# 16-wide attention written out as straight code, with keys and queries turned into planes per group

## The reference

```python
qkv = einsum('bsh,oh->bso', layernorm(x), w_qkv) + b_qkv     # 8 x (4 + 2) x 16
q, k = _rope(q, cos, sin), _rope(k, cos, sin)
scores = einsum('bqhd,bkhd->bhqk', q, k) * SM_SCALE           # SM_SCALE = 1/16
scores = where(mask, scores, finfo.min)                       # block mask; causal at this length
probs = softmax(scores)
ctx = einsum('bhqk,bkhd->bqhd', probs, v)
x = x + einsum('bsh,oh->bso', ctx, w_dense) + b_dense
```

## Time and profile before

| what | before |
|---|---|
| median of 3 runs (lowest, highest) | 3000.42 us (2997.31, 3000.43) |
| the profiled execution | 2997.02 us, span 2995.0 us |
| busy in the span | PE 2652.2 us (89%), PE weight loads 1793.2, DVE 1907.5, ACT 1514.3, POOL 822.2 |
| mean granted PE clock | 0.945 of 2.4 GHz |
| L0a: projection / first minima / groups | 21.3 to 108.8 / 108.8 to 135.5 / 135.5 to 446.5 us |
| L1b: the same | 2148 to 2235.8 / 2235.8 to 2262 / 2262 to 2575.6 us |

### The profile page before, as it was taken

The page is one execution under the profiler, slowest core; times in us unless marked ns, Lnnn a source line. Parts: engine busy times, 40 slices in busy tenths (PEclk is TensorE's granted clock), DMA queues, the critical chain, the costliest instruction groups (busy, mean ns, idle before and its releaser), DMA issues. The chain is left out here.

```text
span 2995.0 us, 46427 instructions
## 1 busy us (share of the span) xinstructions
PE 2652.2 (89%) x14824; PEld 1793.2 (60%) x14886; DVE 1907.5 (64%) x3382; ACT 1514.3 (51%) x2540; POOL 822.2 (27%) x777
## 2 busy tenths in 40 slices
PE   6789988886999999999999987999578888778995
PEld 4444434454888888888888864666344444345663
DVE  5666642444777787777777766677556666166774
ACT  4466661222555555555555541566265666324663
POOL 1200000104343443445335301455120000003552
PEclk9799998997999999999999988999788999979998
DMA  2100000001000000000000023988500000029887
GB/s 76 71 1 0 0 1 16 19 17 46 19 22 22 22 22 18 22 22 26 15 22 25 8 92 135 297 201 199 144 1 1 0 0 0 11 107 322 211 201 197
DMA packets 68154, 196.92 MB, mean 66 GB/s; under 512 B 9040, under 2 KB 9936, under 8 KB 62608
## 3 DMA queue, kind: packets, MB, share of 16 engines
q1 hardware_dynamic: 46928, 145.44, 14.2%
q0 software_dynamic: 21056, 49.30, 8.7%
HBM read 154.33 MB, written 40.37 MB: 65 GB/s over the span
## 5 line engine op out<-in xcount | busy, mean ns | idle before, releaser
L1315 ACT ACTIVATE L1a_ph<-single 128x512 fp32r<-128x512 f32 (+3 forms) x384 | 174.2, 489 | 180.4 <-PE single L1402 179.7
L698 DVE TENSOR_REDUCE L1b_least<-single 128x1 f32<-128x512 f32 (+3 forms) x304 | 191.2, 660 | 107.9 <-PE single L520 75.9
L698 DVE TENSOR_REDUCE L0a_least<-single 128x1 f32<-128x512 f32 (+3 forms) x304 | 191.1, 660 | 106.9 <-PE single L520 75.5
L1456 DVE TENSOR_TENSOR L1a_pl<-single,L1a_ph 128x512 fp32r<-128x512 f32 (+3 forms) x384 | 199.5, 549 | 52.7 <-ACT L1a_ph L1315 52.0
L1472 DVE SCALAR_TENSOR_TENSOR x<-single,L1a_rinv,x 128x512 f32<-128x512 f32 x256 | 189.5, 745 | 58.4 <-PE single L1066 58.4
L1306 ACT ACTIVATE L1a_probs<-pair,L1a_least 128x128 f32<-128x128 f32 (+7 forms) x256 | 190.0, 744 | 72.0 <-DVE L1a_least L1450 70.8
L1450 DVE TENSOR_REDUCE L1a_least<-pair 128x1 f32<-128x128 f32 (+7 forms) x256 | 190.8, 750 | 43.3 <-PE pair L1391 42.6
L1283 POOL TENSOR_TENSOR L1a_swapped<-L1a_swapped,L1a_sin 128x512 f32<-128x512 f32 x80 | 129.8, 1622 | 303.7 <-ACT L1a_swapped L1347 303.7
L409 ACT ACTIVATE L1b_probsT<-pair 128x896 f32<-128x896 f32 (+2 forms) x192 | 151.2, 811 | 67.4 <-PE pair L539 48.1
L409 ACT ACTIVATE L0a_probsT<-pair 128x896 f32<-128x896 f32 (+2 forms) x192 | 151.2, 811 | 65.9 <-PE pair L539 46.5
L1402 PE MATMUL single<-ident,L1a_probs 128*128 128x128 f32 x1152 | 169.0, 274 | 1.4 <-ACT L1a_probs L1306 1.4
(11 more groups left out here) (517 smaller groups left out, 7052.1 us busy)
## 6 DMA issues: line engine op xcount, KB each, us to landing
L1f_wd<-in_L1f_w SPq DMA_DIRECT2D x48, 512.0 KB, 4.3
L1g_wd<-in_L1f_w SPq DMA_DIRECT2D x48, 512.0 KB, 4.2
L1a_raw<-in_L1a_w SPq DMA_DIRECT2D x80, 256.0 KB, 2.6
L1f_store<-in_L1f_w SPq DMA_DIRECT2D x16, 1024.0 KB, 7.9
L1g_store<-in_L1f_w SPq DMA_DIRECT2D x16, 1024.0 KB, 8.4
sum<-L0a_pad_row SPq DMA_DIRECT2D x2, 2304.0 KB, 11.7
sum<-x SPq DMA_DIRECT2D x16, 256.0 KB, 2.9
x<-sum SPq DMA_DIRECT2D x16, 256.0 KB, 4.7
```

What stands on the lines that cost most here:

```text
L698: dve.tensor_reduce(a.least[:, part, qt, first:first + heads], g.bank(4 + f % 2)[:, 0:heads * w].rearrange("p (j k) -> p j k", j=heads), A ...
L1315: act.activation(p_tile(ph, u, i), turned_bank(u, i), ACT.Copy).then_inc(p_high, 1)
L1456: dve.tensor_tensor(p_tile(pl, u, i), turned_bank(u, i), p_tile(ph, u, i).bitcast(F32), ALU.subtract)\
```

## The change

1. **Straight code.** The hardware loops of the groups become Python loops, so every instruction stands in the program with constant operands.
2. **Two rounded parts in place of three bf16 parts.** Queries and keys are held as a float32r (rounded fp32) high part and a float32r rest. In `qs` a head has 64 columns: high, rest, high, two columns for the row extreme, zeros. In `ks` the key has 64 columns: high, high, rest, ones; with 64 zero columns on each side.
3. **Planes per group.** The projection stretch no longer builds or turns any stack. POOL builds `qs`, `ks` for group kv+2 (`build`), PE turns four tiles of two heads at once into bank 7 (`turn_plane`, 4 matmuls of 128 columns) and ACT copies the bank (`plane_copy`, 128x512). Per group and half of the tokens: two planes K, two planes Q, and later two planes M, which are the Q planes again, now with the row extremes in them. So 12 planes a group take the place of the 40-head stacks and the 8 rows.
4. **Whole arrays, zeros in the other half.** A query plane holds two heads, one in each half of the 128 partitions; the key plane for head j has the key in the half j % 2 and zeros in the other, so the matmul picks one head.
5. **Minima and scores.** Fills now take heads (0, 2) and (1, 3) where two fit in a bank, so 40 fills a group in place of 38; the fills stand behind the two score matmuls of their step, and masks are put a matmul later where they can be. The row extreme has two parts in place of three.
6. **First stretch.** The list `START16` has 4 planes, then the 40 fills of group 0 with 14 more planes among them: the other planes of group 0 and those of group 1.

```diff
-            n = max(1, min(GH, HALF // w))
-            out += [(qt, part, j, n, w) for j in range(0, GH, n)]
+            pairs = ((0, 2), (1, 3)) if 2 * w <= HALF else ((0,), (1,), (2,), (3,))
+            out += [(qt, part, heads, w) for heads in pairs]
...
+TURNS_AT = {
+    1: ("M", 0, 0, 1), 3: ("M", 0, 1, 1), 5: ("K", 2, 0, 0), 6: ("K", 2, 1, 0), 8: ("Q", 2, 0, 0), 10: ("Q", 2, 1, 0),
+    13: ("M", 1, 0, 0), 15: ("M", 1, 1, 0), 16: ("K", 2, 0, 1), 18: ("K", 2, 1, 1), 20: ("Q", 2, 0, 1), 22: ("Q", 2, 1, 1),
+}
...
-        self.qkT = sb("qkT", [P, NQK, T], BF16)
+        self.qs = sb("qs", [P, SETS, NT, GH, ROWS16], F32R)
+        self.ks = sb("ks", [P, 2, NT, 3, ROWS16], F32R)
+        self.qT = sb("qT", [P, SETS, 2, T], F32R)
+        self.kT = sb("kT", [P, SETS, 2, T], F32R)
...
+                def build(kv, c):
...
+                    pool.wait_ge(a.roped, (c + 1) * BLK)
...
+                    pool.tensor_tensor(ks[:, :, 0:HD], k, like(1, HD)[:, :, 0, :], ALU.mult).then_inc(a.stack_high, 1)
+                    pool.tensor_tensor(qs[:, :, :, 0:HD], q, like(GH, HD), ALU.mult).then_inc(a.stack_high, 1)
+                    pool.tensor_tensor(ks[:, :, HD:2 * HD], k, like(1, HD)[:, :, 0, :], ALU.mult).then_inc(a.stack_high, 1)
+                    pool.tensor_tensor(qs[:, :, :, 2 * HD:KF], q, like(GH, HD), ALU.mult).then_inc(a.stack_high, 1)
+                    pool.tensor_tensor(qs[:, :, :, KF:KM], like(GH, 2), like(GH, 2), ALU.subtract).then_inc(a.stack_high, 1)
...
+                    pool.tensor_tensor(ks[:, :, 2 * HD:KF], k, ks[:, :, 0:HD].bitcast(F32), ALU.subtract)\
+                        .then_inc(a.stacked, 1)
+                    pool.tensor_tensor(qs[:, :, :, HD:2 * HD], q, qs[:, :, :, 0:HD].bitcast(F32), ALU.subtract)\
+                        .then_inc(a.stacked, 1)
...
+                def plane_copy(kind, kv, p, c):
...
+                    act.wait_ge(a.plane_turned, PLANE[kind, kv, p, c])
+                    act.activation(to, g.bank(7), ACT.Copy).then_inc(a.plane_copied, 1)
...
-                for t in range(NT):
+                for t in range(2, NT):
+                    qkv(t)
                     if t + 2 < NT:
-                        qkv(t + 2)
-                    turn_stack(t)
-                    if t + 4 < NT:
-                        turn_row(t + 4)
-                pe.wait_ge(a.stackT_copied, 5 * NT)
+                        turn_row(t + 2)
...
+                def turn_plane(kind, kv, p, c):
+
+                    bank_7_free((kind, kv, p, c))
...
+                    for i in range(BLK):
...
+                        mm = pe.matmul(g.bank(7)[:, i * P:(i + 1) * P], rows.rearrange("p j d -> p (j d)"), a.ident[:, :],
+                                       start=True, stop=True)
+                    mm.then_inc(a.plane_turned, 1)
...
+                        mm = pe.matmul(outs[n], a.kT[:, b, j % 2, kt * P:(kt + 1) * P],
+                                       a.qT[:, b, j // 2, c * HALF + q:(c + 1) * HALF], start=True, stop=not diagonal)
...
-                with pe.Fori(0, NKV - 1) as kv:
-                    group(kv, True)
-                group(NKV - 1, False)
```

More of the change, by code:

```diff
@@ L209, in groups @@
     return [(c, kt) for c in range(2) for kt in range(0, BLK * (c + 1), 2)]
-FILLS, GROUPS = fills(), groups()
-NF, NG = len(FILLS), len(GROUPS)
-NF0 = sum(f[0] < BLK for f in FILLS)
+GROUPS = groups()
+NG = len(GROUPS)
 NU = NG * GH
@@ L248, in heads16_plan, with next_fill @@
[L248 to L258, removed]
+    left, order, plan = fills(), [], []
+    total, given = sum(len(h) * w for _, _, h, w in left), 0
+    def next_fill(parity):
+        block = [f for f in left if f[0] // BLK == left[0][0] // BLK][:GH]
+        f = next((f for f in block if f[2][0] % 2 == parity), block[0])
+        left.remove(f)
+        order.append(f)
+        return len(order) - 1
@@ new lines, in heads16_plan @@
+    for n in range(NU):
+        i, j = divmod(n, GH)
+        now = []
+        while len(left) > 2 and given + len(left[0][2]) * left[0][3] <= total * (n + 1) / NU:
+            now.append(next_fill((j + 1 + len(now)) % 2))
+            given += len(order[-1][2]) * order[-1][3]
+        plan.append(("seen", i, j, now))
+        if i == 0 and j == 2:
+            plan.append(("values",))
+        if i and j == 1:
+            plan.append(("weigh", i - 1))
+            if i == GROUPS_BEFORE[1]:
+                plan.append(("copy", 0))
+        if n in TURNS_AT:
+            plan.append(("plane", *TURNS_AT[n]))
+        if i == GROUPS_BEFORE[1] and j == 3:
+            plan.append(("turn", 0))
@@ new lines, in heads16_plan, with heads16_start @@
+    plan += [("fill", next_fill(0)), ("weigh", NG - 1), ("copy", 1), ("fill", next_fill(1)), ("turn", 1)]
+    return plan, order
+PLAN16, FILLS = heads16_plan()
+NF = len(FILLS)
+NF0 = sum(f[0] < BLK for f in FILLS)
+def heads16_start():
+    first = [("K", 0, 0, 1), ("K", 0, 1, 1), ("Q", 0, 0, 1), ("Q", 0, 1, 1)]
+    later = [("M", 0, 0, 0), ("M", 0, 1, 0)] + [(k, 1, p, c) for c in range(2) for k in "KQ" for p in range(2)]
+    out = [("plane", k, 0, p, 0) for k in "KQ" for p in range(2)]
+    for f in range(NF):
+        out.append(("fill", f))
+        if f < NF0 and f % 3 == 2 and first:
+            out.append(("plane", *first.pop(0)))
+        if f >= NF0 + 2 and f % 3 == 2 and later:
+            out.append(("plane", *later.pop(0)))
+    return out + [("plane", *p) for p in first + later]
@@ L452, in _ @@
+                for kv in range(NKV):
+                    for s in PLAN16:
+                        if s[0] == "seen":
+                            exponentials(kv, s[1], s[2])
+                        elif s[0] == "plane" and kv + s[2] < NKV:
+                            plane_copy(s[1], kv + s[2], s[3], s[4])
+                        elif s[0] == "copy":
+                            context_copy(kv, s[1])
                 for t in range(NT):
```

484 lines of the change are left out of this document (229 added, 255 removed).

## The result

The changed kernel took 3007.18 us (median of 18 runs, 2996.28 to 3017.53) against 2997.40 us for the kernel before on the same chips: a ratio of 1.0026, 95% interval 1.0015 to 1.0037. It is 0.3% slower, where 2942 us were forecast. Its profiled execution took 3003.43 us (span 3001.7), and by the steps of the sum (2938.5 us for a profiled execution) that is 65 us longer than forecast.

What follows compares the result with a forecast made beforehand. PE was taken as nearest to the bound in the groups. Projection savings less costlier minima and groups gave -27.7 and -30.8 us, so 2997.0 - 58.5 = 2938.5, plus 3.4 to the median: 2942 us, range 2895 to 2985.

Steps and rivals of the forecast that it cites:

- Projection: Before the first fill: tiles 5.6 us apart, then four planes in 5.4 us; first fill 35.5 us earlier in L0a.
- First minima: Group 0's first minima: planes make PE dense enough to raise its clock; 29 us, up from 26.7 (+2.3).
- The bound of 36 us for PE at the lower clock: First minima: columns, masks and planes with loads behind masks would take PE about 36 us at 1.2 GHz.
- Groups: Score groups: PE's work rises from 31.8 to 39.8 us through planes and float32r loads; with waits, period 41.5.
- its own sign: Groups: a period outside 40 to 43.4 us would show the prediction wrong; that forecast case held 0.57.
- group 6: The group without 8 planes: forecast at 38.0 us, against 41.5 for a full group.
- the forecast's 1.7: Waits of PE left in a group, mainly at the end of each half: 1.7 us, down from 7.8.
- my 24.6 (16.6 + 3.5 + 4.5): PE's work in a group: 72 x 0.23 for columns, 64 masks, 56 float32r loads behind masks at 0.08.
- The term for masks: Groups: 64 masks at 3.5 us, plus 4.5 us for 56 places where a float32r matmul follows a mask.
- the old 7.8 us of waits: Groups of the kernel before: 39.55 us period less 31.8 of PE's work, called waits and loop register instructions.
- Waits stay: Rival for the groups, chance 0.14: bank 7's strict turns keep waits; period 43.5 to 45.4, time 2972 to 2999 us.
- The projection does not shrink so: Rival, chance 0.05: planes, POOL's clearing or a low clock through the minima return 15 us a block; 2957 to 2975.

Runs made afterwards that it cites:

- The experiment with added matmuls: Changed kernel plus unread PE matmuls behind the last projection tile, the four lone planes and each fill of the first minima: 2976.86 us, ratio 0.9910.
- The straight version: Kernel before with its group loops on PE, ACT, DVE and GpSimd written out as straight code, nothing else changed: 2975.86 us, ratio 0.9908.
- the quiet version in three parts: Changed kernel's order with q and k in three bf16 parts, 10 planes a group, without added matmuls: 2936.86 us (one run).

## Why the prediction was wrong, step by step

**Projection: right but for the clock.** Tiles came 5.6 us apart (30.13 to 68.88 in seven steps, the last 0.45 shorter), and the four planes stood where I put them. At the lower clock they are 1.8 us apart in place of 1.35, and the first bias is 1.9 us late; 1.7 us a block and 1.9 once were missed.

**First minima: the step that failed.** I wrote that "with the planes PE is dense enough at the lower clock to bring it up", from one row where the clock rose at 3.90 of 4 us. It did not rise at 3.91 nor, in an experiment, at 4.00, and a window of the kernel before (132 to 136 us) had shown the same. That, and not a size, was wrong, and it made 12.9 us a block here, and 2.0 in group 0, which began at the lower clock (118.7 to 164.17 is 45.5 us, a group at full clock 43.5). The experiment with added matmuls puts the whole of the clock at 15.4 us in L0a. The bound of 36 us for PE at the lower clock was too low as well: the stretch took 41.9, with PE busy 38.1 of 40.9. Why the clock did not come back is open; float32r fills are not the reason, since it stayed down with bf16 fills too.

**Groups: the mechanism was right, two terms were too small.** PE bounds the group, as forecast, and float32r's loads and the planes are what it pays for. The period was 43.47 and not 41.5, just outside the 40 to 43.4 that the prediction gave as its own sign. Of the 16.4 us a block, 9.9 are five such groups at 2.0, 4.0 are group 0 (its low clock among them), 2.5 are group 6 (40.5 for 38.0), and the last is as forecast (29.6). From starts in one period: weighing 8.6 (forecast 8.9), planes 5.5 (5.3), context turns 0.8 (1.0), and 28.6 for fills, scores and masks. In these 28.6 some starts are late by a wait, by about 2.6 us together (the view of waits shows 1.3 of it, since it leaves out the load that follows a wait), against the forecast's 1.7. The other 26.0 stand against my 24.6 (16.6 + 3.5 + 4.5). The term that the sum put at nothing is the float32r load that shows behind what is not a mask: 12 planes, 6 weighings and 2 context turns. An example is 226.13 to 226.64 on PE's timeline, two score matmuls of 512 columns behind a plane: 0.51 us, not 0.46. The term for masks was too dear by itself, as the run without masks showed, so the two errors partly cancel; how they divide to a tenth of a microsecond is open.

**What the old 7.8 us of waits were.** I took the kernel before as 31.8 us of work and 7.8 of waits. The straight version shows 37.74, so 1.8 of them were the loop. In it PE is busy 34.45 us with 2.4 us of named waits: some of the 7.8 was work that my distances between starts did not hold, and a change could not win it. Then the change against the straight kernel costs 43.47 - 37.74 = 5.7 us a group, of which float32r makes 3.6 (39.85 with bf16 arrays). The other 2.1 are left for planes in place of rows, 40 fills for 38 and the new order, which no run separates. Over the 12 groups with all their planes, and 2.7 in each group 6 (40.47 for 37.73), that is 74 us, and the straight code gives 25 back.

**The balance against the kernel before**, from its marks (first score at 138.3 and 2264.8, both worked out from the mask behind it; last normalisation at 446.5 and 2575.6) and the earlier trace rows: from first bias to first fill or reduce 80.5 to 46.7 us in L0a and 82.0 to 47.7 in L1b, -68.1; from there to the first score 29.5 to 41.9 and 28.8 to 40.8, +24.4; to the last normalisation 308.2 to 332.9 and 310.8 to 332.8, +46.7; the first bias +1.9, outside the blocks +1.8. The sum is +6.7, and the spans differ by 3001.7 - 2995.0 = 6.7.

**The rivals.** "Waits stay" named this period almost exactly (43.5 to 45.4), but for another reason, so that is luck: no wait on a plane copy is in the group's waits after. "The projection does not shrink so", with the clock low through the minima, got 0.05 and was what happened there. I held the two as cases that exclude each other. Both came, and their sum crosses zero.

## What to carry to other kernels

A stretch in which PE waits a few times for one single buffer can cost much more than its waits, if PE is the bound behind it: look at the granted clock of the stretch behind, and price PE at the lower level unless a row of the same mix of matmuls shows it rising. Fewer parts are no fewer passes as long as the rows fit in 128: here three bf16 parts and two float32r parts take the same columns, and float32r pays some 0.06 us more at each of 76 weight loads. Compare stretches by the same two marks in both kernels: 26.7 us and 28.8 us were the same first minima. When a change has several parts, run each alone: the straight code alone gave 0.9%, which the rest of the change spent.

## What the runs showed of the hardware

- The clock fell with PE busy 2.09 of 4 us, and at 3.47 of 4 us in one block while the same program held it at 3.11 in the other (L0a, 88 to 92 us). It stayed at 0.50 at 4.00 of 4 us in float32r fills and at 3.75 in bf16 fills, but rose behind 3.92 of 4 us with six bf16 matmuls of 512 columns, and in the quiet version in three parts at 2.90 and 3.03. The busy share of PE does not decide it by itself.
- In the hardware loop ACT loads its table once a turn, 1.28 us; in straight code once a block (14 loads against 2).
- Eighteen matmuls of 512 columns that nobody reads, 4 us of PE's time ahead of L0a's first minima, made these 13 us shorter (40.8 to 27.8). In L1b the same program lost the clock within the minima, and they were 5.5 us shorter (40.8 to 35.3).
